# Causal attention with relative positions: products reordered, the mask moved from TensorE to GpSimd

## The reference, cut to what matters

```python
def _skew(QEr):                      # (B, H, R, C)
    padded = jnp.pad(QEr, ((0, 0), (0, 0), (0, 0), (1, 0)))
    return padded.reshape(B, H, C + 1, R)[:, :, 1:, :]

QEr  = jnp.einsum('bhsd,ld->bhsl', q, Er)
attn = (jnp.einsum('bhsd,bhtd->bhst', q, k) + _skew(QEr)) / math.sqrt(16)
attn = jnp.where(causal, attn, -jnp.inf)
out  = jnp.einsum('bhst,bhtd->bhsd', softmax(attn), v)
```

## Time and profile before

| | |
|---|---|
| Median of the runs | 1255.08 us (1251.07 to 1260.55, 3 runs) |
| Profiled execution | 1249.16 us, span 1247.4 us |
| PE, DVE, ACT busy in the span | 1084.9, 659.5, 637.8 us |
| POOL busy in the span | 199.1 us |
| Causal attention | from about 57 us (first `psE` product) to about 406 us (last division) |
| L538 `psS<-dmask,identb` | 256 matmuls, 219 ns median |
| L603 `PT<-psT` | 100.2 us in all |
| L596 `scores<-psS,bias` and `<-psS,x` | 176 and 80 instructions, 284 to 692 ns |

### The profile page before, as it was taken

The page is one execution under the profiler, slowest core; times in us unless marked ns, Lnnn a source line. Parts: engine busy times, 40 slices in busy tenths (PEclk is TensorE's granted clock), DMA queues, the critical chain, the costliest instruction groups (busy, mean ns, idle before and its releaser), DMA issues. The chain is left out here.

```text
span 1247.4 us, 21976 instructions
## 1 busy us (share of the span) xinstructions
PE 1084.9 (87%) x6978; PEld 670.0 (54%) x6979; DVE 659.5 (53%) x1993; ACT 637.8 (51%) x1245; POOL 199.1 (16%) x466
## 2 busy tenths in 40 slices
PE   7879999999997869899999995447999999997487
PEld 4435555555554549899998894212333333334344
DVE  4416767777764661121111110866766666684697
ACT  2427667667642323223322221425777777763687
POOL 0000000000000011133222220002222322240232
PEclk9957999999979889899999998668999999998699
DMA  5077887787743843677666662464111111110001
GB/s 177 1 278 276 299 296 280 274 295 275 279 168 136 322 158 120 229 228 226 230 227 218 212 207 78 155 198 122 46 49 44 45 48 45 45 33 9 0 29 41
DMA packets 75343, 199.55 MB, mean 160 GB/s; under 512 B 7881, under 2 KB 40905, under 8 KB 69257
## 3 DMA queue, kind: packets, MB, share of 16 engines
q1 hardware_dynamic: 71528, 188.45, 44.8%
q0 software_dynamic: 3744, 10.23, 2.1%
HBM read 134.82 MB, written 63.83 MB: 159 GB/s over the span
## 5 line engine op out<-in xcount | busy, mean ns | idle before, releaser
L766 DVE CUSTOM_DVE_ANT_0 unused<-mpsS,mask_bias 128x512 bf16<-128x512 f32 x256 | 172.0, 691 | 82.9 <-PE mpsS L699 82.5
L1507 ACT ACTIVATE hT<-ph,w 128x128 f32<-128x128 f32 x312 | 89.2, 368 | 207.1 <-PE ph L1481 207.1
L793 ACT ACTIVATE mPT<-mpsB 128x512 f32<-128x512 f32 x256 | 152.7, 597 | 80.9 <-PE mpsB L706 74.4
L1481 PE MATMUL ph<-xT,w 128*128 128x128 f32 x1248 | 152.4, 282 | 6.9 <-DMA w<-in_w1p 6.8
L1481 PEld LDWEIGHTS ph<-xT,w 128*128 128x128 f32 x1248 | 147.8, 198 | 9.6 <-issue 8.9
L1526 DVE TENSOR_TENSOR xn<-py,b 128x256 f32<-128x256 f32 x39 | 16.6, 425 | 246.5 <-PE py L1491 246.5
L1491 PE MATMUL py<-w,hT 128*128 x624 | 141.2, 379 | 0.7 <-DVE xn L1526 0.7
L634 ACT COPY stage<-psE 128x1024 f32<-128x1024 f32 (+1 forms) x96 | 83.6, 871 | 93.1 <-PE psE L524 90.3
L641 ACT ACTIVATE scores<-scores,nm 128x512 f32<-128x512 f32 (+3 forms) x256 | 125.2, 554 | 7.9 <-DVE nm L609 7.9
L596 DVE CUSTOM_DVE_ANT_0 scores<-psS,bias 128x512 f32<-128x512 f32 (+3 forms) x176 | 77.7, 487 | 88.4 <-PE psS L538 88.1
L1491 PEld LDWEIGHTS py<-w,hT 128*128 128x128 f32 x624 | 115.6, 190 | 15.2 <-issue 1.1
(11 more groups left out here) (251 smaller groups left out, 1610.6 us busy)
## 6 DMA issues: line engine op xcount, KB each, us to landing
rel<-stage SPq DMA_DIRECT2D x64, 640.0 KB, 4.2
w<-in_w1p SPq DMA_DIRECT2D x39, 1028.0 KB, 5.7
bias<-rel SPq DMA_DIRECT2D x44, 640.0 KB, 4.4
x<-rel SPq DMA_DIRECT2D x20, 640.0 KB, 4.8
mqk<-packed SPq DMA_DIRECT2D x64, 192.0 KB
w<-in_w2p SPq DMA_DIRECT2D x8, 1024.0 KB, 12.7
b<-in_b SPq DMA_DIRECT2D x39, 128.0 KB, 5.9
got<-pair_out SPq DMA_DIRECT2D x8, 512.0 KB, 8.9
```

The costliest lines, as they stand in the source:

```text
L766: nc.vector.tensor_tensor_reduce(out=unused[:, i, :], in0=psS[i % 2][:, :], in1=mask_bias[:, i, :], scale=1.0, scalar=-3.0e38, op0=ALU.add ...
L793: nc.scalar.activation(PT[r][:, j, :], psB[j % 2][:, :], ACT.Exp, scale=1.0 / 4).then_inc(s_exp, 1)
L1481: mm = nc.tensor.matmul(ph[half][:, q * P:(q + 1) * P], w1[i][:, dk * F + f * P:dk * F + (f + 1) * P], xT[i][:, dk, :], start=(dk == 0), s ...
L1507: g = nc.scalar.activation(hT[i][:, f, :], ph[half][:, q * P:(q + 1) * P], ACT.Gelu, bias=w1[i][:, DK * F + f:DK * F + f + 1])
```

## The change

- `rel` and `stage` get one more column for each head (`REL_P` = 1281). VectorE sets it to -2^100 once.
- `hide` is gone: 256 matmuls. Every score product now starts and stops its own accumulation.
- TensorE's order within a unit is `relative`, `score`, `turn_probs`, and then one `weigh` call after unit 0 and one after unit 1. The `turn` stays at the end.
- GpSimd writes -2^100 into the first 128 columns of each of the four blocks of `stage`, left of the anti-diagonal, with `affine_select`. After the skewed read these places stand above the diagonal. An instruction covers two blocks of one head (128 x 256 elements, in place), four for each pair, 128 in all. GpSimd waits for the third copy of a pair, and SyncE's write of a head waits for that head's two selects.
- GpSimd's spreading of values stands behind the selects in its queue, once in two iterations.
- The write's rows are 5124 bytes long, 5120 before; the skewed read steps by 5120 bytes, 5116 before.

```diff
--- before.py
+++ after.py
@@ -60,10 +60,11 @@
     packed = dram("packed", (PIECES, B, D, 2, S), BF16)
 
     REL_W = sum(w for unit in CAUSAL_UNITS for _, _, w in unit)
+    REL_P = REL_W + 1
 
     x_rows = dram("x_rows", (TOK, D), F32)
     pair_out = dram("pair_out", (TOPK * TOK + SLOT_TILES * P, D), F32)
-    rel = [dram(f"rel_{r}", (P, REL_W), F32) for r in range(ROUND)]
+    rel = [dram(f"rel_{r}", (P, REL_P), F32) for r in range(ROUND)]
 
     with top:
         def sem(name):
@@ -440,7 +441,7 @@
             last = NP + GROUP
             kf = xnT
             with ExitStack() as ctx:
-                stage = [sb(ctx, f"stage{r}", [P, 2, REL_W]) for r in range(2)]
+                stage = [sb(ctx, f"stage{r}", [P, 2, REL_P]) for r in range(2)]
                 bias = [sb(ctx, f"bias{r}", [P, 2, REL_W]) for r in range(2)]
                 bias.append(x[:, :, :].rearrange("p t d -> p (t d)")[:, 0:2 * REL_W].rearrange("p (a w) -> p a w", a=2))
                 scores = [sb(ctx, f"scores{r}", [P, 2, REL_W]) for r in range(3)]
@@ -454,8 +455,8 @@
                 s_wr = [sem(f"s_wr{r}") for r in range(ROUND)]
                 s_rd = [sem(f"s_rd{r}") for r in range(ROUND)]
                 s_back = sem("s_back")
-                names = ("emm", "eev", "smm", "soft", "nm", "exp", "tmm", "tev", "seen", "seensp")
-                s_emm, s_eev, s_smm, s_soft, s_nm, s_exp, s_tmm, s_tev, s_seen, s_seen_sp = (
+                names = ("emm", "eev", "smm", "soft", "nm", "exp", "tmm", "tev", "seen", "seensp", "cut", "edge", "seenpool")
+                s_emm, s_eev, s_smm, s_soft, s_nm, s_exp, s_tmm, s_tev, s_seen, s_seen_sp, s_cut, s_edge, s_seen_pool = (
                     sem(f"s_{n}") for n in names)
                 block = ctx.enter_context(nc.Block())
 
@@ -489,12 +490,14 @@
                             sp.sem_inc(s_seen_sp, 1)
                             if p >= len(bias):
                                 sp.wait_ge(s_soft, piece(p - len(bias), NU - 1, h) + 1)
-                            skewed = bass.AP(rel[slot].ap().tensor, P - 1, [[REL_W - 1, P], [1, REL_W]])
+                            skewed = bass.AP(rel[slot].ap().tensor, P - 1, [[REL_P - 1, P], [1, REL_W]])
                             sp.dma_start(bias[p % len(bias)][:, h, :], skewed).then_inc(s_rd[slot], 16)
 
                     def write(p):
-                        sp.wait_ge(s_eev, NU * (p + 1))
+                        if p == 0:
+                            sp.wait_ge(s_edge, 2)
                         for h in range(2):
+                            sp.wait_ge(s_cut, 2 * (2 * p + h + 1))
                             slot = (2 * p + h) % ROUND
                             wait(sp, s_rd[slot], 16 * (2 * p // ROUND))
                             sp.dma_start(rel[slot][:, :], stage[p % 2][:, h, :]).then_inc(s_wr[slot], 16)
@@ -528,15 +531,9 @@
                     def score(p, u):
                         for h in range(2):
                             wait(pe, s_soft, piece(p, u, h) - 1)
-                            for at, (i, off, w) in enumerate(units[u]):
-                                nc.tensor.matmul(psS[:, h, off:off + w], query(p, h, i), key(p, h, w),
-                                                 start=(at == 0), stop=False)
-
-                    def hide(p, u):
-                        for h in range(2):
-                            for at, (i, off, w) in enumerate(units[u]):
-                                mm = nc.tensor.matmul(psS[:, h, off + w - P:off + w], identb[:, :], dmask[:, :],
-                                                      start=False, stop=(at == len(units[u]) - 1))
+                            for i, off, w in units[u]:
+                                mm = nc.tensor.matmul(psS[:, h, off:off + w], query(p, h, i), key(p, h, w),
+                                                      start=True, stop=True)
                             mm.then_inc(s_smm, 1)
 
                     def turn_probs(p, u):
@@ -554,18 +551,16 @@
 
                     for n in range(-REL, last + 1):
                         early, soft, late = (pair_at(n, k) for k in (REL, SOFT, 0))
+                        g, half = divmod(n - 2, 2)
                         for u in range(NU):
-                            if soft is not None:
-                                score(soft, u)
                             if early is not None:
                                 relative(early, u)
                             if soft is not None:
-                                hide(soft, u)
+                                score(soft, u)
                             if late is not None:
                                 turn_probs(late, u)
-                        g, half = divmod(n - 2, 2)
-                        if 0 <= g < NBH // GROUP:
-                            for j in (2 * half, 2 * half + 1):
+                            if 0 <= g < NBH // GROUP and u < 2:
+                                j = 2 * half + u
                                 at, w = key_place[j]
                                 vals.weigh(pe, g, g % 2, j, s_tev, NU * 2 * (g + 1),
                                            lambda h: PT[(2 * g + h // 2) % 4][:, h % 2, at:at + w])
@@ -574,6 +569,8 @@
 
                 @block.vector
                 def _(dve):
+                    for i in range(2):
+                        nc.vector.memset(stage[i][:, :, REL_W:], NEG).then_inc(s_edge, 1)
                     vals.clear(dve)
 
                     for n in range(-SOFT, last + 1):
@@ -611,9 +608,20 @@
 
                 @block.gpsimd
                 def _(pool):
-                    pool.wait_ge(vals.s_zero, 3)
-                    for g in range(NBH // GROUP):
-                        vals.spread_values(pool, g, g % 2)
+                    keep = dict(base=-(P - 1), channel_multiplier=1, compare_op=ALU.is_ge, fill=nc.gpsimd.to_reg(NEG))
+                    for n in range(-REL, NP):
+                        if (p := pair_at(n, REL)) is not None:
+                            rows = stage[p % 2]
+                            pool.wait_ge(s_eev, NU * (p + 1))
+                            pool.sem_inc(s_seen_pool, 1)
+                            for h in range(2):
+                                for first in (rows[:, h, 0:1024].rearrange("p (u c) -> p u c", c=512)[:, :, 0:P],
+                                              rows[:, h, 896:1152].rearrange("p (u c) -> p u c", c=P)):
+                                    nc.gpsimd.affine_select(out=first, in_=first, pattern=[[0, 2], [1, P]], **keep).then_inc(s_cut, 1)
+                        if n == 0:
+                            pool.wait_ge(vals.s_zero, 3)
+                        if n >= 0 and n % 2 == 0:
+                            vals.spread_values(pool, n // 2, n // 2 % 2)
 
                 @block.scalar
                 def _(act):
```

## The result

| | before | changed |
|---|---|---|
| Median | 1250.73 us (20 runs, 1241.03 to 1260.55) | 1257.59 us (20 runs, 1252.09 to 1262.40) |
| Ratio | | 1.0071, 95% interval 1.0051 to 1.0091 |
| Span of the profiled execution | 1247.4 us | 1259.7 us |
| PE, DVE, ACT, POOL busy | 1084.9, 659.5, 637.8, 199.1 us | 1048.6, 662.0, 631.7, 246.1 us |

39 us were to be saved, and 7 were lost. PE has 36 us less busy time, so the work did go. What follows the causal attention takes about as long as before: the last `nm` of the causal attention comes 12.9 us later, the end of the span 12.3 us.

A forecast was written before the change was run, and what follows sets the result against it. It took TensorE and VectorE, waiting for each other by turns, to bound the kernel. Savings of 31 + 1 + 2 + 2.5 + 2.5 = 39 us from the median 1255.1 gave 1216 us, range 1203 to 1240.

The forecast's parts named there:

- What bounds the kernel now: Full iterations: TensorE and VectorE wait by turns; 0.63 + 0.69 us of each is TensorE at a quarter of its row groups.
- The compute: Full iterations laid out by hand: 7.81 us odd, 8.17 even, mean 7.99 for 9.29 to 9.32, with VectorE setting the period.
- The sum of 39 us: Whole kernel's saving: 31 us in full iterations, 1 + 2 + 2.5 + 2.5 us around them.
- Its main term: Iterations n=2 to 26: 33.8 us gained, 2.5 taken off for missed waits, leaving 31 us.
- the one on the transfers: SyncE's queue: 7.4 us of DMA work covered in 8.0 us; ScalarE's wait, 7.1 to at most 9.0 us, within 9.9.
- the signs by which the prediction wanted to be called wrong: ScalarE waits for a write, clock under 1.00 between 120 and 320 us, or value products not fitting under VectorE's chain.
- another wait takes the place of those removed, for instance ScalarE's for its write: Full iterations: period stays at 9.3 us, only part of the 8 us around them comes, about 1250 us; chance 0.07.
- The price of the 5124-byte rows: SyncE's writes: same price as before taken; up to 0.55 us more for a pair would still cost nothing.
- The rival on it asked for writes 1.3 to 1.5 times dearer in DMA work: DMA engines become the bound: 1227 us at 1.3 times, 1247 at 1.5; chance 0.15.
- The rival on it expected a falling clock from the missing mask products alone: TensorE's clock falls in full iterations, some 4 us each, 1316 us with all 25; chance 0.06.
- GpSimd: Selects: 0.6 us each, 2.4 for a pair, of 8 available, costing nothing on TensorE's path.
- The ends: Around full iterations: 1 us in n=0 and 1, 2 in n=-2 and -1, 2.5 in n=27 to 29, 2.5 in n=30 and 31.

The follow-up runs named there:

- write first: The changed kernel with SyncE's write of pair n+5 ahead of the reads of pair n+4: 1212.03 us, ratio 0.9728 to the kernel before.

## Why the prediction was wrong

**What bounds the kernel now: right as far as the engines go.** TensorE and VectorE did wait for each other by turns, and the time in which only one group of rows works was there to be had.

**The compute: right, once it can show.** TensorE in the kernel with write first and rows of 5184 bytes, one odd and one even iteration:

```profile
204.19 0.70 PE L527 MATMUL psE<-er,ctxT 32*128 32x512 f32 x2
...
206.85 0.60 PE L527 MATMUL psE<-er,ctxT 32*128 32x384 f32 x2
...
209.55 0.48 PE L527 MATMUL psE<-er,ctxT 32*128 32x256 f32 x2
...
211.30 0.66 PE L549 MATMUL psT<-ident,scores 128*128 128x128 f32 x4 [0.44 <-DVE PT L600]
211.89 0.70 PE L527 MATMUL psE<-er,ctxT 32*128 32x512 f32 x2
...
215.05 0.60 PE L527 MATMUL psE<-er,ctxT 32*128 32x384 f32 x2
...
217.96 0.48 PE L527 MATMUL psE<-er,ctxT 32*128 32x256 f32 x2
...
219.12 0.66 PE L549 MATMUL psT<-ident,scores 128*128 128x128 f32 x4 [0.44 <-DVE PT L600]
```

From the start of unit 0, the odd n has unit 1 at 2.66, unit 2 at 5.36, the last transpositions at 7.11 and its end at 7.70; predicted were 2.65, 5.26, 7.23 and 7.81. The even n has 3.16, 6.07 and 7.23 for 3.10, 5.96 and 7.16. The transpositions wait for VectorE's copy, as forecast. The changed kernel does so too between its stalls. The signs named for this are there: writes 7.95 us apart, 8.2 and 7.7 by turns, DVE busy for 0.85 of the stage, and a DMA share of 0.90. The sum of 39 us is also met in size: 1250.7 x (1 - 0.9679) = 40 us. Its main term is too: from n=2 to n=26 the `nm` instructions span 191.1 us for 223.1, which is 32 us in 24 iterations.

**The step that failed is the one on the transfers.** The prediction compared the DMA engines' work of a pair, 7.4 us, with 8.0 us, and called what lay between covered, with 2.5 us taken off. That is a comparison of throughput. In SyncE's queue a pair's work is a chain: issue the write, wait for it to land, issue the read, and only then the next write. Its length was in the timeline of the kernel before: 4.7 us from a write to the second read, then both reads. The cycle needs 7.9 us of work and about 2 us in which the DMA engines have nothing to do. This is an estimate from the changed kernel: 0.79 of the 10.05 us between two `nm` instructions is 7.9. I had listed the read in the queue behind the write and asked whether the bias came in time. I had not asked what stands behind the read: the next write, and through the stage buffer ScalarE. For its wait the prediction allowed 9.9 us and put 7.1 to 9.0 against it, with nothing for the time the write stands in line; it lands 8.4 us after an issue that had itself been held by the landing before. That ScalarE waits for a write was one of the signs by which the prediction wanted to be called wrong: it waits 76 us of 230. A clock under 1.00 was another. The rival "another wait takes the place of those removed, for instance ScalarE's for its write" named the right place, with a chance of 0.07; it took the period to stay at 9.3 us, and it grew to 10.2.

**The price of the 5124-byte rows was the second mistake.** "I take the same price" was justified by bytes. The bytes are nearly the same, but without selects the period was 0.35 us longer than with rows of 5120 (10.12 and 9.77), and in the old kernel the rows alone made the difference between a queue that waits and one that is waited for. The rival on it asked for writes 1.3 to 1.5 times dearer in DMA work and so missed how little was needed. By the runs: rows alone in the old kernel +1.3%, rows of 5184 in the changed one -0.55%. It is not the main step: with the odd rows and the write first 0.9728 was reached.

**What came on top is the clock.** It is 0.90 where TensorE stands still for 44 of 230 us. The rival on it expected a falling clock from the missing mask products alone. With the new order, the queue free and the same products missing it is 0.99 and 1.00, so in this order the waits are needed for it to fall. But the rival had seen something: where the queue is the bound, the kernels without mask products have the lower clock (0.90 for 0.96, 0.83 for 0.97), and with the old order it is 0.94 even with the write first. What the clock costs by itself no run took apart.

**GpSimd: right.** A select took 0.41 us against the 0.6 taken. The estimate of 2.56 us from the Trainium skill, "GPSIMD Engine Reference", section 3.1, on loops that branch on data, was not met; at the 1.2 GHz of that estimate 407 ns for 256 elements are 1.9 cycles each, and fit the 1 to 2.6 cycles of the same section. Of the rows that the prediction named beside it, 479 ns for 256 columns fit too, but 722 ns for 272 are 3.2 cycles. **Change of kind on TensorE:** small, as taken: in the last timeline four transpositions take 0.59 us up to the next score and relative products (211.30 to 211.89).

**The ends: right in part.** From n=26 to n=29 the changed kernel gained 7.3 us where 2.5 had been forecast. Without new relative products ScalarE waits for no write there, and the granted clock in this stretch was 0.87 for 0.75 before, which the forecast had left as it was.

Open: whether the dear part of the odd rows is the write or the read that steps with it, what keeps the kernel before from queueing its writes behind the reads, and how much of each loss is the clock. That selects alone in the old order (1.0147) are slower than selects with masks (1.0099) is itself not certain, as the intervals overlap.

## What to carry to other kernels

Before a change makes an iteration shorter, follow each queue once around: what it issues, what it waits for, and what stands behind that wait. If a queue's own chain is as long as the iteration, the gain ends there however idle the engines behind it look; the sum of its work says nothing on it. A write that waits for nothing but data should not stand behind a read that waits for an earlier write to land. A row padded by one element is worth a run with more padding: here 64 bytes instead of 4 took back most of the loss where the queue was the bound.

## What the runs showed of the hardware

- DMA writes from SBUF to DRAM with rows of 5124 bytes landed in 4.4 us at the median where each waited for the reads to land, those with rows of 5120 in 4.2 in the kernel before, where they follow the second read by 3.9 us at the median (1.7 to 5.4). Behind two reads it was 8.4 and 8.0 us, and the period of the chain 10.12 and 9.77 us. Where this chain is the bound, 5184 bytes were better than 5124 (ratios 1.0016 and 1.0071).
- A pair of writes issued 0.4 us after the second of two 640 KB reads landed after 7.4 and 8.9 us; in the kernel before a write landed in 4.2 us at the median.
- With a free order the DMA engines ran at a share of 0.92, 323 GB/s of mixed reads and writes.
- `affine_select` on 128x256 fp32, in place: 407 ns.
- Where SyncE's queue was the bound, the granted clock from 120 to 320 us was 0.97 and 0.96 with 256 short mask products in the stage, and 0.83 and 0.90 without them.
